# Reordering the steps of a selective scan's pair on VectorE, with four state buffers and new places for the work beside it

## What is computed

```python
def _selective_scan(u, delta, A, Bm, Cm, Dv):
    def step(h, inps):
        u_t, dt, B_t, C_t = inps
        dA = jnp.exp(dt[:, :, None] * A)
        h = dA * h + (dt * u_t)[:, :, None] * B_t[:, None, :]
        y = jnp.einsum('bdn,bn->bd', h, C_t) + Dv * u_t
        return (h, y)
...
xl = jnp.concatenate([flat, flat, flipped, flipped], axis=1)   # 4 x 192 channels
delta = softplus(dt_r @ W_delta + b_delta)
y = _selective_scan(xl, delta, A, Bm, Cm, Dp)
```

## Time and profile before

| | us |
|---|---|
| median of three runs | 22490.82 |
| lowest and highest of them | 22447.25, 22503.70 |
| the profiled execution: time | 22505.68 |
| the profiled execution: span, first to last instruction | 22503.9 |
| busy in it: DVE / PE / ACT / POOL | 19251.1 / 18818.0 / 15624.5 / 6356.1 |
| mean granted TensorE clock (1 is 2.4 GHz) | 0.894 |

### The profile page before, as it was taken

One profiled execution on the slowest core, in us unless ns is written; L12 is line 12 of the kernel. 1 busy time (PEld: TensorE's weight loads), 2 busy tenths in 40 slices (PEclk: granted clock), 3 DMA queues, 4 the chain that ended last, 5 costly groups with the idle time before them and its releaser, 6 DMA issues.

```text
span 22503.9 us, 334261 instructions
## 1 busy us (share of the span) xinstructions
PE 18818.0 (84%) x100834; PEld 6890.1 (31%) x100834; DVE 19251.1 (86%) x17938; ACT 15624.5 (69%) x21098; POOL 6356.1 (28%) x3909
## 2 busy tenths in 40 slices
PE   5888888888888888888888888888888888888887
PEld 1333333333333333333333333333333333333332
DVE  4888888888888888888888888888888888888887
ACT  3767777777677677776776777767767767777674
POOL 1222222222222222222222222222222222222222
PEclk8889898898898998988988889889889898898898
DMA  5555555555555555555555555545555555555552
GB/s 144 143 135 140 140 138 139 135 144 137 132 142 138 137 142 135 143 138 134 140 141 133 140 136 141 140 133 143 138 133 143 139 139 141 134 142 136 134 141 75
DMA packets 1418366, 3083.16 MB, mean 137 GB/s; under 512 B 207812, under 2 KB 786696, under 8 KB 1407859
## 3 DMA queue, kind: packets, MB, share of 16 engines
q1 hardware_dynamic: 1372146, 2992.85, 51.6%
q10 hardware_dynamic: 44032, 64.26, 1.1%
HBM read 2796.25 MB, written 221.51 MB: 134 GB/s over the span
## 4 chain that ended last, share of the span: by engine, by line
issue 67%; POOL 15%; PE 8%; DVE 5%; ACT 4%; DMA 1%; POOLq 0%; ACTq 0%; SPq 0%; DVEq 0%
POOL drive L1576 13%; PE bank L575 3%; DVE state L1381 3%; PE state_sum L575 2%; PE pair L575 2%; POOL taps L1563 2%; ACT work L920 1%; DVE drive L1237 1%; PE scan_sum L575 1%; ACT L920 0%; ACT decay_even L920 0%; DVE work L1237 0%; ACT du L920 0%; DVE prod L1237 0%; ACT decay L920 0%
## 5 line engine op out<-in xcount | busy, mean ns | idle before, releaser
L1576 POOL TENSOR_TENSOR drive<-du,Bb 128x784 f32<-128x784 f32 x3072 | 5689.7, 1852 | 15638.6 <-DVE drive L1237 15638.6
L575 PE MATMUL state_sum<-state,fold 128*64 128x392 f32 x24576 | 5610.5, 585 | 1052.4 <-DVE state L1381 1029.9
L1381 DVE TENSOR_TENSOR_SCAN state<-decay_even,drive 128x784 f32<-128x784 f32 x3072 | 5500.2, 1790 | 128.4 <-ACT decay_even L920 17.6
L1381 DVE TENSOR_TENSOR_SCAN state<-decay,drive 128x784 f32<-128x784 f32 x3072 | 5473.3, 1782 | 0.2 <-POOL drive L1576 0.2
L920 ACT ACTIVATE decay_even<-delta,alog 128x784 f32<-128x784 f32 x3072 | 2821.6, 918 | 3240.8 <-DVE state L1381 3224.0
L1237 DVE TENSOR_TENSOR prod<-state_sum,Cb 128x784 f32<-128x784 f32 x3072 | 2950.6, 960 | 1906.4 <-PE state_sum L575 1902.4
L575 PE MATMUL scan_sum<-prod,fold 128*64 128x392 f32 x12288 | 2990.4, 568 | 1500.0 <-DVE prod L1237 1493.9
L575 PEld LDWEIGHTS state_sum<-state,fold 128*64 128x64 f32 x24576 | 1706.4, 154 | 4427.8 <-issue 2288.4
L575 PE MATMUL bank<-rep,taps 120*32 120x392 f32 x30720 | 2973.9, 514 | 96.1 <-ACT image L920 33.8
L920 ACT ACTIVATE decay<-delta,alog 128x784 f32<-128x784 f32 x3072 | 2890.3, 941 | 115.6 <-issue 72.7
L1237 DVE TENSOR_TENSOR drive<-du,Bb 128x784 f32<-128x784 f32 x3072 | 2943.0, 958 | 18.9 <-DVE work L1237 11.9
(11 more groups left out here) (169 smaller groups left out, 17504.8 us busy)
## 6 DMA issues: line engine op xcount, KB each, us to landing
Bb<-bc_rows SPq DMA_DIRECT2D x3072, 392.0 KB, 4.4
rep<-expanded_images SPq DMA_DIRECT2D x3840, 168.0 KB
Cb<-bc_rows SPq DMA_DIRECT2D x3072, 196.0 KB, 3.6
expanded_images<-image SPq DMA_DIRECT2D x1152, 112.0 KB, 2.5
rep<-conv_in_images SPq DMA_DIRECT2D x1152, 112.0 KB, 3.9
dwo<-in_pww SPq DMA_DIRECT2D x65, 1152.0 KB, 7.3
conv_in_images<-image SPq DMA_DIRECT2D x384, 112.0 KB, 3.2
xc<-xc ACTq DMA_DIRECT2D x384, 98.0 KB, 2.6
```

Of the source, the lines that this page charges most:

```text
L575: return pe.matmul(out, lhsT, rhs, start=start, stop=stop)
L1381: v.tensor_tensor_scan(state[:, j % STATES, :], DP[:, 0:L] if j % 2 == 0 else decay[:, j // 2 % DECAYS, :], drive[:, j % 2, :], 0.0, ALU.m ...
L1576: pool.tensor_tensor(drive[:, j % 2, :], du[:, 2 * s + r, :], Bb[:, b % BSLOTS, :], ALU.mult).then_inc(drive_r.sem, 1)
```

## The change

What it does:

- VectorE's order in a pair becomes: even scan, work beside, odd scan, even drive of the next pair, product of the pair behind, work beside. At the end of a period the drive is that of the next sample's first pair.
- STATES goes from 3 to 4.
- TensorE's order becomes: fold, work beside, summation of the pair behind, work beside.
- ScalarE issues, for pair j/2, the odd decay, a visit at place j-2, the even decay, a visit at place j-1; the first pair's two decays stand ahead of the loop, and the last turn of a period makes those of the next sample's first pair.
- The places of the head and of the tail are written anew: convolution slots, far deltas, the mixing of the experts behind the first deltas, the readings, and most steps of `post`, `mixer`, `ffn` and `attention` by about one place.
- Small steps: the gate's bias seb2 is added by a matmul with the identity instead of by VectorE (scp is gone); the group norm's power, formerly on GpSimd, is a logarithm and an exponential on ScalarE, and its shift a ScalarE copy; seT2 shares storage with wdl; dbl moves by one slot of dwo; SyncE's loads of the C rows move by one place.

The diff, cut to its core:

```diff
-STATES = 3
+STATES = 4
...
-CONV_SLOTS = (1, 2, 3, 5, 7, 8, 9, 10, 11, 12, 13, 14, 15, 17, 18, 19, 20, 21, 23, 24, 26)
+CONV_SLOTS = (1, 2, 3, 4, 6, 7, 9, 10, 11, 13, 14, 15, 16, 17, 18, 19, 20, 21, 23, 24, 26)
...
-             ("mix", 0): 79.1, ("mix", 1): 80.3, ("dbl",): 81.1,
-             ("delta", 0, 0): 84.3, ("delta", 0, 1): 85.1, ("delta", 1, 0): 86.3, ("delta", 1, 1): 87.1})
-FAR = {("delta", m, h): slot(k) + SECOND * h for m, k in ((2, 4), (3, 6), (4, 16), (5, 22)) for h in range(2)}
+             ("dbl",): 81.1, ("delta", 0, 0): 84.3, ("delta", 0, 1): 85.1, ("delta", 1, 0): 87.1, ("delta", 1, 1): 89.1,
+             ("mix", 0): 91.1, ("mix", 1): 93.1})
+FAR = {("delta", m, h): slot(k) + SECOND * h for m, k in ((2, 8), (3, 12), (4, 22), (5, 25)) for h in range(2)}
...
-READ_AT = {name: at + 1.8 for name, at in HEAD.items()}
+READ_AT = {name: at + (2.4 if name[0] in ("conv", "conv3", "mix") else 1.8) for name, at in HEAD.items()}
...
 # SyncE, c_rows
-                    yield 4 * q - 3.4 if q > 1 else 0.9
+                    yield 4 * q - 2.4 if q > 1 else 2.0
...
 # TensorE, scan
                 for p in range(NP):
-                    if p >= 1:
-                        summation(i, p - 1)
-                    elif later(i):
-                        summation(i - 1, NP - 1)
-                    go_on(between, 2 * p + 1)
                     pe.wait_ge(state_r.sem, state_r.at(i, 2 * p + 2))
...
                     last.then_inc(folded.sem, 1)
                     go_on(between, 2 * p + 2)
+                    if p >= 1:
+                        summation(i, p - 1)
+                    elif later(i):
+                        summation(i - 1, NP - 1)
+                    go_on(between, 2 * p + 3)
...
 # ScalarE, scan
-                for j in range(0, NU, 2):
-                    decaying(j, DP[:, 0:L], 2, even_r)
-                    go_on(between, j - 1.5)
-                    odd(j + 1)
-                    go_on(between, j - 1)
+            def scan(i, ahead, *between):
+                for j in range(2, NU + 2 if ahead else NU, 2):
+                    for n in (j + 1, j):
+                        if n < NU:
+                            decaying(i, n)
+                        else:
+                            decaying(i + 1, n - NU)
+                        go_on(between, j - 2 if n > j else j - 1)
...
 # ScalarE, gating
-                yield 2.95 + 2 * b
+                yield 3.6 + 2 * b
...
 # VectorE, scan
+                if not later(i):
+                    driving(i, 0)
                 for p in range(NP):
-                    driving(2 * p)
                     scanning(2 * p)
+                    go_on(between, 2 * p)
+                    scanning(2 * p + 1)
+                    if p < NP - 1:
+                        driving(i, 2 * p + 2)
+                    elif ahead:
+                        driving(i + 1, 0)
                     if p >= 1:
                         product(i, p - 1)
                     elif later(i):
                         product(i - 1, NP - 1)
-                    go_on(between, 2 * p)
-                    scanning(2 * p + 1)
                     go_on(between, 2 * p + 1)
```

More of the change, by code:

```diff
@@ L103 @@
+READ_AT.update({("hidden",): 54.5, ("gate",): 56.5, ("dbl",): 83.9, ("delta", 0, 0): 86.0, ("delta", 0, 1): 87.0, ("delta", 1, 0): 89.0, ("delta", 1, 1): 91.0})
 READ_AT.update({("delta", m, h): AT["delta", m, 0] + (1.4, 1.8)[h] for m in range(NEAR, NK) for h in range(2)})
-LOG_AT = {0: (88.6, 90.5, 91.0), 1: (88.7, 90.6, 93.0)}
+LOG_AT = {0: (87.6, 88.6, 91.0), 1: (91.6, 92.6, 94.0)}
 LOG_AT.update({m: (AT["delta", m, 0] + 3.4, AT["delta", m, 0] + 5.4, AT["delta", m, 0] + 6.9) for m in range(NEAR, NK)})
@@ L388, in build, with decay_of @@
         lmax = w[2][:, 8:8 + NB]
+        def decay_of(j):
+            return decay[:, j // 2 % DECAYS, :] if j % 2 else DP[:, 0:L]
         def u_of(m):
@@ L634, in head @@
                 for n in range(2 * T0):
-                    last = mm(P[0:RHID, 0:1], seT1[:, n // 2, :], ssum[:, n:n + 1], start=n == 0, stop=n == 2 * T0 - 1)
+                    last = mm(P[32:32 + RHID, 0:1], seT1[:, n // 2, :], ssum[:, n:n + 1], start=n == 0, stop=n == 2 * T0 - 1)
                 last.then_inc(bank_filled.sem, 1)
@@ L1058, in far_logs, with decaying @@
                     yield from log_of(i, m)
[L1060 to L1078 removed]
+            def decaying(i, j):
+                s, m, r = PAIRS[j // 2]
+                k, n = 2 * s + r, 2 * m + j % 2
+                exponentials()
+                if m == 0:
+                    act.wait_ge(dl_r.sem, dl_r.at(i, k + 1))
+                back, signal = (2 * DECAYS, odd_r) if j % 2 else (2, even_r)
+                if j >= back or later(i):
+                    act.wait_ge(state_r.sem, state_r.at(i, j - back + 1))
+                ac(decay_of(j), delta[:, k, :], ACT.Exp, scale=alog[:, k, n:n + 1]).then_inc(signal.sem, 1)
+            def scan(i, ahead, *between):
[6 more added lines that the diff above has]
+                        go_on(between, j - 2 if n > j else j - 1)
                 go_on(between, END)
@@ L1310, in head @@
             def head(i, span):
-                yield 55
-                v.wait_ge(bank_filled.sem, bank(span, "gate"))
-                tt(scp[:, :], P[:, 0:T0], seb2[:, :], ALU.add).then_inc(bank_read.sem, 1)
-                yield 57
-                v.wait_ge(sc_r.sem, sc_r.at(i))
+                yield 58
+                v.wait_ge(bank_read.sem, bank(span, "gate"))
                 tt(wpw[:, :, :], pwm[:, :].rearrange("p (t c) -> p t c", t=T0), sc[:, :].unsqueeze(2).to_broadcast([128, T0, C]),
@@ L1354, in steps, with scan @@
                     tt(du[:, m, :], delta[:, m, :], u_of(m), ALU.mult).then_inc(du_r.sem, 1)
-            def scan(i, *between):
+            def scan(i, ahead, *between):
                 def product(i, p):
@@ L1380, in scanning @@
                     v.wait_ge(drive_r.sem, drive_r.at(i, j + 1))
-                    v.tensor_tensor_scan(state[:, j % STATES, :], DP[:, 0:L] if j % 2 == 0 else decay[:, j // 2 % DECAYS, :], drive[:, j % 2, :], 0.0,
+                    v.tensor_tensor_scan(state[:, j % STATES, :], decay_of(j), drive[:, j % 2, :], 0.0,
                                          ALU.mult, ALU.add).then_inc(state_r.sem, 1)
@@ L1528, in _ @@
             go_on([Beside(lead(0, (FIRST, 0))), Beside(shares(1))], END)
-            scan(0, Beside(steps(0, NEAR, NK)), Beside(lead(1, (LOOP, 0))), Beside(shares(2)))
+            scan(0, True, Beside(steps(0, NEAR, NK)), Beside(lead(1, (LOOP, 0))), Beside(shares(2)))
             done = SETUP_LINKS + 2 * LEAD_LINKS
```

167 lines of the change are left out of this document (81 added, 86 removed).

## The result

The changed kernel takes 22832.84 us, the median of four runs (22755.47 to 22862.46), against 22477.33 for the kernel before in the same setting: a ratio of 1.0153 with a 95% interval of 1.0124 to 1.0183. It is slower by 1.5%, where 6% faster was forecast. The profiled execution has a span of 22847.1 us, 343 more than before, at a mean granted clock of 0.896 (0.894 before).

What follows compares the result with a forecast made beforehand. VectorE and TensorE were taken as coupled too tightly, the product waiting for the fold, to even out their loads. Per period 30.95-4-4-2 = 21 us, over 64 periods 1344; 22503.9-1344 gives 21160 us, range 20500 to 22450.

Steps and rivals of the forecast that it cites:

- The wait and its mechanism: VectorE's product waits 1902.4 us for TensorE's fold; moved to the pair's end, permitted lateness 3.5 us instead of 1.3.
- rival C: TensorE's longer gaps draw its clock down, making the kernel slower; 23080 us at clock 0.74; chance 0.13.
- the drive a half pair earlier: VectorE's even drive moved; GpSimd's odd drive behind it keeps 2.75 us of cover, so cost taken at 0.
- ScalarE's excess: Gates apart from expansions add six table loads per period, delaying even decays: 0 to 5.3 us per period, taken 4.
- run 21 us per period ahead: Not a run: the forecast's net gain per period over the whole loop, 30.95-4-4-2 = 21 us.
- the bound of 30.95 us: Greatest gain per period if in each of ten slices only the busier of VectorE and TensorE counted: 314.05 against 345.
- the 1344: Forecast gain in us over the whole run: 21 per period over 64 periods.
- Rival B: Product's wait moves and half returns, ScalarE and chains add costs: gain 8 us per period, 21990 us; chance 0.17.
- the port: Not in the prediction; the experiments' suspect: VectorE's visit behind the product, whose steps stand until GpSimd's odd drive ends.
- the small steps: Gate's bias to TensorE, power to ScalarE, next sample's first decays made ahead: tenths of a microsecond off the path, 0.
- new places of head and tail: Mixing of the experts and far deltas move later: same work elsewhere, taken at 0; tail chains separately cost 2 us.
- The four state buffers: With four, the next even scan need not wait for the fold to finish reading a state; taken at 0.

Runs made afterwards that it cites:

- one_visit: The changed kernel without VectorE's visit behind the product, its steps falling to the next visit between the scans: 22569.98 us, 1.0037 of the kernel before.
- pool_half: The changed kernel with GpSimd's odd drive cut to the first 392 of its 784 positions, nothing moved: 22644.03 us, 1.0061 of the kernel before.
- gates_back: The changed kernel with ScalarE's three gates at their former places, sharing visits with expansions: 22699.39 us, 1.0098 of the kernel before.
- both: The changed kernel with the edits of one_visit and gates_back together: 22212.99 us, 0.9877 of the kernel before.
- both_bare: The kernel both with two bare waits of VectorE, for ScalarE's copies, one pair later: 22249.27 us, 0.9885 of the kernel before.
- both_nosilu: The kernel both with every Silu replaced by an Identity, leaving ScalarE almost without table loads: 21603.61 us, 0.9606 of the kernel before.
- order_only: The kernel before with VectorE's and TensorE's new orders, four state buffers and the few moves these need: 22788.43 us, 1.0124 of the kernel before.
- both_rot: The kernel both with three decay buffers (one PSUM, two SBUF) going round over all scans: 22760.83 us, 1.0111 of the kernel before.

## Why the prediction was wrong

**The wait and its mechanism: right.** The product's wait fell under 600 us (431.9), scan_sum's vanished, TensorE's wait ahead of state_sum became one for the product, loads rose by 373, and the clock stayed at 0.896. So rival C, the only slower one, is not what happened: it had the sign, by a mechanism that did not occur.

**The step that failed first: the drive a half pair earlier, taken at 0.** Its working asked whether GpSimd's odd drive has cover, and it has: the odd scan waits 0.2 us for it. It did not ask what GpSimd's drive runs beside. With the product moved to the end of the pair, the work beside that follows it lies within the 1.85 us of GpSimd's drive, and its steps stand still until that ends: 606 us of VectorE's busy time by one_visit, 616 by pool_half. In time it is worth 263 us taken alone, and with the gates cured as well 486 (gates_back to both). The bound on the slices' sum rested on VectorE's 300.10 us per period staying what it is.

**The second: ScalarE's excess, taken at 4 us per period.** The count of loads was right, and so, nearly, was the part that was worked out: at the fourth and fifth pairs, where the gates fell apart, VectorE waits 5.7 us per period for the even decay, against an upper bound of 5.3. What the sum left out is the rest. The even decay's wait, forecast at some 250 us in the first five pairs, was 554.9, with 188 in later pairs, and over all of its steps VectorE waits 1184 us more for ScalarE than before, 18.5 per period. The working treated the slack of the even decay as its own; but the gain asks VectorE to run 21 us per period ahead of where it ran, and every result of ScalarE that had been early by less than that is then late; this reading is argued from the sums, not shown by one run. gates_back shows the part that belongs to the switches: 348 us of wait, 133 of time alone, 357 with the visit cured (one_visit to both). An activation begins 1.29 us after its load here too (10149.03 behind 10147.74), and the next load 0.02 us behind that activation's end (10149.73 behind 10149.71). So the drain that the Trainium skill adds to the load at every switch (ScalarE: Activation LUTs, section "What ACT_TABLE_LOAD costs") is not to be seen and not the cause. The Trainium skill's advice to batch by table set (ScalarE: Activation LUTs, section "Table sets: the hidden batching unit") is what gates_back follows, and the runs agree with that by 133 us.

**The third: the bound of 30.95 us, of which nearly all was taken.** It lets each slice last as long as its busier engine, as if no tie but that of fold and product were left. Even with both costly parts cured the gain is 284 us, and 401 with ScalarE freed of its loads: a fifth and three tenths of the 1344. TensorE's wait for the product stays above 2100 us in all these kernels. both_bare shows why a sum of waits overstates: removed at one tie, they return at the next. Rival B had that mechanism and 22 us of its own per period; it missed the port as well, so its 21990 is below what even both reaches.

**Two readings of the earlier trace rows that don't hold.** One of the two engines is within 3 us of full in five of the ten slices, not in most. And against rival C it is said that the granted clock is 1.00 in slices where TensorE is nearly full: the ninth, its fullest with 32.81 of 34.5, reads 0.88. Neither enters the sum; the second took from an argument against C, which did not happen.

**What stays open**: which tie holds the last 1000 us, of TensorE's fold and product, the chains through the pair tile (643 us in both, the largest entry), and the even decay. The even decay alone is not enough: in both_nosilu VectorE waits 18.3 us for it, and the time is still 444 above the forecast. The rotation of the buffers would have told them apart, but for the port.

**Taken at 0, and near it**: the small steps and the new places of head and tail. Together with ScalarE's visits half a pair apart they make the difference from order_only to the changed kernel, 0.3% with intervals that overlap; each by itself was not measured. The four state buffers are in both of these kernels, so no run prices them; no scan of the changed kernel shows a wait for TensorE to free a state.

## What to carry to other kernels

Before an instruction is moved, ask what will run beside it, and beside the steps that follow it, on an engine that can hold these up, not only who waits for it: here a step's length doubled without any wait in the profile, and only the means by shape showed it. A wait that the profile puts at 1900 us is worth that much only if nothing else is nearly as late; remove it on paper and see which result is then late next, on every engine, and take off its price too. And of work that can wait, put it neither ahead of what another engine is waiting for nor beside a GpSimd instruction that holds it up.

## What the runs showed of the hardware

A VectorE step with two SBUF inputs, or a cast of f16 to fp8, that begins while GpSimd runs its 1.85 us product of two SBUF tensors does not slow down in proportion; it stands until GpSimd's instruction ends: 1.33 us for 0.33 (cast), 2.77 for 1.77 (scan). From that end it takes a fixed time, some 0.12 us less than its usual length: 0.22 us for the cast, whether GpSimd's instruction takes 1.86 us (the changed kernel) or 1.02 (pool_half), and 1.65 for the scan (both_rot). The same scan with its decay in PSUM, and the product with one input in PSUM, are not held (1.77 and 0.96). The profile counts the standing as busy time.
